# Delta rule in a decoder layer: products of raw keys, key norms applied as row and column factors

## The reference

```python
mixed = silu(causal_conv1d(hidden @ w_qkv, conv_w))
q, k, v = split(mixed)
q, k = l2norm(q), l2norm(k)              # x * rsqrt(sum(x*x) + 1e-6), per token and head
beta, g = sigmoid(b), -exp(A_log) * softplus(a + dt_bias)
for t in range(512):                     # per batch and value head, S is 128 x 128
    S = S * exp(g_t)
    delta = (v_t - k_t @ S) * beta_t
    S = S + outer(k_t, delta)
    o_t = (q_t * 128**-0.5) @ S
core = o * rsqrt(mean(o*o) + 1e-6) * norm_weight * silu(z)
x = x + core @ w_out
```

## Time and profile before

| | |
|---|---|
| median of 3 runs | 3336.58 us (3334.99 to 3337.07) |
| the profiled execution, its own time | 3335.47 us |
| its span in the profile | 3333.6 us |
| instructions | 59535 |
| busy TensorE (PE) | 3238.8 us, 97% of the span |
| busy VectorE (DVE) | 2414.8 us, 72% |
| busy GpSimd (POOL) | 1863.5 us, 56% |
| busy ScalarE (ACT) | 1541.4 us, 46% |
| DMA, mean | 70 GB/s |

### The profile page before, as it was taken

One profiled execution on the slowest core, in us unless ns is written; L12 is line 12 of the kernel. 1 busy time (PEld: TensorE's weight loads), 2 busy tenths in 40 slices (PEclk: granted clock), 3 DMA queues, 4 the chain that ended last, 5 costly groups with the idle time before them and its releaser, 6 DMA issues. The chain is left out here.

```text
span 3333.6 us, 59535 instructions
## 1 busy us (share of the span) xinstructions
PE 3238.8 (97%) x20832; PEld 2152.7 (65%) x20832; DVE 2414.8 (72%) x3622; ACT 1541.4 (46%) x4983; POOL 1863.5 (56%) x1824
## 2 busy tenths in 40 slices
PE   5899999999999999999999999999988999999999
PEld 2577777777777777777777777777764444454444
DVE  6799999999999999999999999999940011034453
ACT  2455556555655555556555655565631000011232
POOL 2677777777777777777777777777740000011132
PEclk8999999999999999999999999999989999999999
DMA  2122322323232323322332233223215222211001
GB/s 101 42 61 77 70 71 58 77 64 71 64 77 64 71 65 71 73 65 61 78 71 69 58 78 67 67 66 77 75 52 211 76 101 101 76 38 64 0 13 38
DMA packets 373958, 231.85 MB, mean 70 GB/s; under 512 B 290304, under 2 KB 323200, under 8 KB 368128
## 3 DMA queue, kind: packets, MB, share of 16 engines
q1 hardware_dynamic: 372368, 220.97, 25.4%
q10 hardware_dynamic: 1296, 7.08, 0.5%
HBM read 156.39 MB, written 71.57 MB: 68 GB/s over the span
## 5 line engine op out<-in xcount | busy, mean ns | idle before, releaser
L722 PE MATMUL acc<-xT,wc 128*128 128x512 f32 x2048 | 935.8, 600 | 2.8 <-PEq L111 2.0
L722 PEld LDWEIGHTS acc<-xT,wc 128*128 128x128 f32 x2048 | 370.2, 191 | 373.2 <-issue 372.5
L1007 DVE SCALAR_TENSOR_TENSOR d_conv<-acc,wc,d_conv 128x511 f32<-128x511 f32 (+2 forms) x768 | 567.0, 738 | 42.7 <-ACT d_conv L1176 33.5
L735 PE MATMUL acc<-wc,xT 128*128 128x256 f32 x2048 | 473.4, 384 | 0.0
L735 PEld LDWEIGHTS acc<-wc,xT 128*128 128x128 f32 x2048 | 379.1, 190 | 46.2
L622 POOL TENSOR_TENSOR d_bf<-d_kks,d_gam 128x512 f32<-128x512 f32 x128 | 160.3, 1273 | 317.9 <-ACT d_kks L1222 317.9
L1530 PE MATMUL acc<-t_area 128*128 128x512 f32 x768 | 332.5, 592 | 1.0 <-ACT t_area L1979 1.0
L1035 DVE STREAM_TRANSPOSE d_em<-d_dm 128x1024 f16<-128x1024 f16 x256 | 314.5, 1229 | 2.2
L2036 POOL TENSOR_SCALAR t_veps<-t_mv 128x1 f32<-128x1 f32 x32 | 9.7, 303 | 546.1 <-DVE t_mv L1775 546.1
L1042 DVE TENSOR_TENSOR d_zm<-d_tz,cons 128x512 f16<-128x512 f32 x384 | 259.1, 675 | 52.7 <-PE d_tz L790 47.7
L1765 DVE TENSOR_TENSOR t_x<-acc,t_x 128x512 f32<-128x512 f32 x16 | 11.1, 692 | 392.4 <-PE acc L1530 392.4
(11 more groups left out here) (227 smaller groups left out, 7084.5 us busy)
## 6 DMA issues: line engine op xcount, KB each, us to landing
d_decay<-decay_rows SPq DMA_DIRECT2D x64, 512.0 KB, 5.2
v_rows<-d_vb SPq DMA_DIRECT2D x256, 128.0 KB, 2.3
d_vn<-v_rows SPq DMA_DIRECT2D x64, 512.0 KB, 3.6
core_rows<-d_ob SPq DMA_DIRECT2D x1024, 32.0 KB, 1.7
t_area<-core_rows SPq DMA_DIRECT2D x30, 1024.0 KB, 4.8
wc<-in_w SPq DMA_DIRECT2D x96, 256.0 KB, 3.3
t_x<-in_x SPq DMA_DIRECT2D x4, 1024.0 KB, 9.6
t_area<-in_wout ACTq DMA_DIRECT2D x2, 2048.0 KB, 13.4
```

The lines of the kernel that those rows point to most:

```text
L722: last = nc.tensor.matmul(bank(TILE[j])[:, :], wtile(j, k), xT[:, k, r % B * S:(r % B + 1) * S], start=k == 0, stop=k == KT - 1)
L735: last = nc.tensor.matmul(bank(f"z{j}")[:, i * GV * P:(i + 1) * GV * P].rearrange("p (h n) -> p h n", h=GV), xT[:, k, r % B * S + (2 * j + ...
L1007: nc.vector.scalar_tensor_tensor(c[:, d:S], bank(TILE[j])[:, 0:S - d], tap(j, KS - 1 - d), c[:, d:S], ALU.mult, ALU.add).then_inc(taps, 1)
```

## The change

It lets the keys be used raw where they stand with channels on partitions, and puts the norms in afterwards:

- silu writes raw keys straight into `kT`, which has four buffers now; `k_turn` reads them there. `normal_k` still makes `khat` (for `grow`). `khat_turn` and `copy_kT` are gone.
- `kk` and `kq` are products of raw keys. Their copies out of PSUM are four of 128 columns, each scaled per row by `rk` (four buffers now), in place of one of 512 columns without a scale.
- B needs the norm of the column's token too. SP stores `rk` to DRAM (`store_row`) and loads it back to all 128 partitions as a row of 512 (`load_row`, 256 KB), and GpSimd multiplies `kks` by it in place (`column_scale`) ahead of `b_full`.
- `read_k` uses raw keys, so GpSimd makes `rt` = -decay times `rk` (`state_scale`, 128 x 8), which `residual` takes as its factor.
- TensorE's order: `kk` of unit n stands where `kq` of unit m stood, and `kq` where `khat_turn` stood. The place of `kk`, between `grow` and `level_d(m, 3)`, is empty. ScalarE's order: `copy_kk` stands where `copy_kq` stood, and `copy_kq` where `copy_kk` stood. The banks follow.

```diff
@@ -320,9 +320,9 @@
         cb, decay, ident = many("conv", 2, [P, S]), many("decay", 2, [P, GV, S]), sb("ident", [P, S])
-        kraw, vraw, vn = sb("kraw", [P, S]), sb("vraw", [P, GV, S]), many("vn", 2, [P, NC, GV * NC, 32])
+        krow, vraw, vn = sb("krow", [P, S]), sb("vraw", [P, GV, S]), many("vn", 2, [P, NC, GV * NC, 32])
         khat = many("khat", 2, [P, S])
-        qT, kT = many("qT", 3, [P, S]), many("kT", 3, [P, S])
+        qT, kT = many("qT", 3, [P, S]), many("kT", 4, [P, S])
         tabm = many("tabm", 4, [P, QN * GV * NC])
...
@@ -429,12 +430,12 @@
 
-        RING_ORDER = ("q", "k", "z1", "v1", "k_turn", "z0", "kq", "v0", "khat_turn", "q_turn", "kk")
-        RING_BANK = {"q": 1, "k": 2, "z1": 0, "v1": 1, "k_turn": 2, "z0": 0, "kq": 2, "v0": 0, "khat_turn": 2, "q_turn": 2, "kk": 1}
+        RING_ORDER = ("q", "k", "z1", "v1", "k_turn", "z0", "kk", "v0", "kq", "q_turn")
+        RING_BANK = {"q": 1, "k": 2, "z1": 0, "v1": 1, "k_turn": 2, "z0": 0, "kq": 1, "v0": 0, "q_turn": 2, "kk": 2}
         RING_FREED = {"k": (taps, "taps", 2), "q": (taps, "taps", 5), "v0": (taps, "taps", 8), "v1": (taps, "taps", 11),
                       "z0": (z_silued, "z_silued", 0), "z1": (z_silued, "z_silued", 1),
-                      "k_turn": (khat_ready, "squares", NC - 1), "khat_turn": (kT_ready, "once", 0), "q_turn": (q_squares, "squares", NC - 1),
-                      "kk": (kk_copied, "once", 0), "kq": (kqs_ready, "once", 0)}
+                      "k_turn": (khat_ready, "squares", NC - 1), "q_turn": (q_squares, "squares", NC - 1),
+                      "kk": (kk_copied, "squares", NC - 1), "kq": (kqs_ready, "squares", NC - 1)}
         CONV_ORDER = ("k", "v1", "v0", "q")
...
@@ -494,8 +495,12 @@
                     next_weights(n, 3)
+                if project:
+                    store_row(n)
                 if invert:
                     store_v(back(n, 1))
+                if project:
+                    load_row(n)
                 if recur:
...
@@ -546,6 +551,15 @@
 
+            def store_row(n):
+                sp.wait_ge(rk_ready, at(n, 2, 2))
+                sp.dma_start(row_dram[n[1] % 2], rk[n[1] % 4][:, :]).then_inc(row_moved, 16)
+
+            def load_row(n):
+                sp.wait_ge(row_moved, at(n, 32, 16))
+                wait(sp, kk_ready, count(n, 1))
+                sp.dma_start(krow[:, :], bc(row_dram[n[1] % 2].rearrange("p c -> (p c)"), P, 0)).then_inc(row_moved, 16)
+
             def store_o(s):
...
@@ -579,7 +593,19 @@
                 wait(pool, khat_ready, at(back(n, 1), NC, NC))
-                nc.gpsimd.tensor_tensor(rk[:, :], rkt[:, :], cons[:, C_POW:C_POW + NC], ALU.pow).then_inc(rk_ready, 1)
+                nc.gpsimd.tensor_tensor(rk[n[1] % 4][:, :], rkt[:, :], cons[:, C_POW:C_POW + NC], ALU.pow).then_inc(rk_ready, 1)
+
+            def state_scale(n):
+                pool.wait_ge(tab_ready, count(n))
+                pool.wait_ge(rk_ready, at(n, 2, 2))
+                nc.gpsimd.tensor_tensor(rt[n[1] % 4][:, :].rearrange("p (h c) -> p h c", h=GV),
+                                        tab(n, Q_NEGDEC).rearrange("p (h c) -> p h c", h=GV), bc(rk[n[1] % 4][:, :], GV),
+                                        ALU.mult).then_inc(rt_ready, 1)
+
+            def column_scale(n):
+                pool.wait_ge(kk_copied, at(n, NC, NC))
+                pool.wait_ge(row_moved, at(n, 32, 32))
+                nc.gpsimd.tensor_tensor(by_chunk(kks), by_chunk(kks), krow[:, :].rearrange("p (i c) -> p c i", c=NC), ALU.mult).then_inc(kk_ready, 1)
 
...
@@ -616,13 +642,13 @@
             def b_full(n, h):
-                pool.wait_ge(kk_copied, count(n))
+                pool.wait_ge(kk_ready, count(n))
                 pool.wait_ge(gams_ready, nth(n, "gams_ready", h))
                 wait(pool, bl_ready, nth(n, "bl_ready", h, 1))
                 nc.gpsimd.tensor_tensor(bf[h][:, :], kks[:, :], gam[h][:, :], ALU.mult).then_inc(bf_ready, 1)
 
             def p_full(m, h):
-                pool.wait_ge(kqs_ready, count(m))
+                pool.wait_ge(kqs_ready, at(m, NC, NC))
                 pool.wait_ge(gamc_ready, nth(m, "gamc_ready", h))
...
@@ -689,12 +715,14 @@
                     k_norm(n)
+                    state_scale(n)
                 if finish:
                     o_norm(f)
                     o_gate(f, 0)
                     o_gate(f, 1)
                 if project:
                     gate_strict(n, 0)
+                    column_scale(n)
                     b_full(n, 0)
...
@@ -750,12 +778,7 @@
                 ring_free(n, "k_turn")
-                turn(bank("k_turn"), kraw, k_turned)
-
-            def khat_turn(n):
-                pe.wait_ge(khat_ready, at(n, NC, NC))
-                ring_free(n, "khat_turn")
-                turn(bank("khat_turn"), khat[n[1] % 2], khat_turned)
+                turn(bank("k_turn"), kT[n[1] % 4], k_turned)
 
...
@@ -763,15 +786,15 @@
             def kk(n):
-                pe.wait_ge(kT_ready, count(n))
+                pe.wait_ge(silued, nth(n, "silued", 0))
                 ring_free(n, "kk")
-                products(bank("kk"), kT[third(n)], kT[third(n)], kk_done)
+                products(bank("kk"), kT[n[1] % 4], kT[n[1] % 4], kk_done)
 
             def kq(m):
-                pe.wait_ge(kT_ready, count(m))
+                pe.wait_ge(silued, nth(m, "silued", 0))
                 pe.wait_ge(silued, nth(m, "silued", 1))
                 ring_free(m, "kq")
-                products(bank("kq"), kT[third(m)], qT[third(m)], kq_done)
+                products(bank("kq"), kT[m[1] % 4], qT[third(m)], kq_done)
 
...
@@ -963,15 +986,16 @@
                     head_start(s, 1)
+                if project:
+                    kk(n)
+                if invert:
+                    level_z(m, 2)
+                if project:
+                    tile(n, 2)
+                if invert:
+                    level_d(m, 2)
                 if invert:
                     kq(m)
-                    level_z(m, 2)
-                if project:
-                    tile(n, 2)
-                if invert:
-                    level_d(m, 2)
-                if project:
-                    khat_turn(n)
                 if recur:
...
@@ -983,8 +1007,6 @@
                     head_start(s, 4)
-                if project:
-                    kk(n)
                 if invert:
...
@@ -1063,7 +1085,8 @@
                 dve.wait_ge(ks_s, at(s, 3, c))
-                nc.vector.scalar_tensor_tensor(by_block(chunk(rr, h)), by_block(chunk(psa, h)), tab(s, Q_NEGDEC, h, c),
+                dve.wait_ge(rt_ready, count(s))
+                nc.vector.scalar_tensor_tensor(by_block(chunk(rr, h)), by_block(chunk(psa, h)), rt[s[1] % 4][:, h * NC + c:h * NC + c + 1],
                                                vn[s[1] % 2][:, :, h * NC + c, :], ALU.mult, ALU.add).then_inc(r_ready, 1)
...
@@ -1178,11 +1201,11 @@
                 if j == 0:
-                    wait(act, k_turned, count(n, 1))
+                    wait(act, ks_s, at(back(n, 4), 3, 3))
                 if j >= 2:
                     wait(act, v_flipped, count(n, 1))
                 v = vraw
-                out = (kraw[:, :], qT[third(n)][:, :], v[:, 0, :], v[:, 1, :])[j]
+                out = (kT[n[1] % 4][:, :], qT[third(n)][:, :], v[:, 0, :], v[:, 1, :])[j]
                 nc.scalar.activation(out, conv_of(TILE[j])[:, :], ACT.Silu).then_inc(silued, 1)
...
@@ -1207,10 +1230,6 @@
 
-            def copy_kT(n):
-                act.wait_ge(khat_turned, count(n))
-                nc.scalar.activation(kT[third(n)][:, :], bank("khat_turn")[:, :], ACT.Copy).then_inc(kT_ready, 1)
-
             def b_high(n, h):
...
@@ -1218,8 +1237,10 @@
                 act.wait_ge(kk_done, count(n))
+                act.wait_ge(rk_ready, at(n, 2, 2))
                 wait(act, bf_ready, at(back(n, 1), GV, GV))
-                nc.scalar.activation(kks[:, :], bank("kk")[:, :], ACT.Copy).then_inc(kk_copied, 1)
+                for c in range(NC):
+                    nc.scalar.activation(chunk(kks, c), chunk(bank("kk"), c), ACT.Copy, scale=rk[n[1] % 4][:, c:c + 1]).then_inc(kk_copied, 1)
 
...
@@ -1232,12 +1253,13 @@
                 for c in range(NC):
-                    nc.scalar.activation(chunk(khat[n[1] % 2], c), chunk(bank("k_turn"), c), ACT.Copy, scale=rk[:, c:c + 1]).then_inc(khat_ready, 1)
+                    nc.scalar.activation(chunk(khat[n[1] % 2], c), chunk(bank("k_turn"), c), ACT.Copy, scale=rk[n[1] % 4][:, c:c + 1]).then_inc(khat_ready, 1)
 
             def copy_kq(m):
                 act.wait_ge(kq_done, count(m))
                 wait(act, p_ready, at(back(m, 1), GV, GV))
-                nc.scalar.activation(kqs[:, :], bank("kq")[:, :], ACT.Copy).then_inc(kqs_ready, 1)
+                for c in range(NC):
+                    nc.scalar.activation(chunk(kqs, c), chunk(bank("kq"), c), ACT.Copy, scale=rk[m[1] % 4][:, c:c + 1]).then_inc(kqs_ready, 1)
 
...
@@ -1318,18 +1340,17 @@
```

(16 more changed lines are left out.)

11 lines of the change are left out of this document (6 added, 5 removed).

## The result

The changed kernel takes 3342.43 us in the median of 19 runs (3340.01 to 3343.75), the kernel before 3334.57 in 19 runs beside them (3330.95 to 3338.97). The ratio is 1.0022, with an interval from 1.0015 to 1.0029: slower, as forecast, by 0.22%, and inside the range. The size is not what was forecast: +7.9 us measured, where the sum had +13.3.

A forecast was written before the change was run, and what follows sets the result against it. TensorE was taken to bound the kernel, with VectorE 2.7 us behind in a slot. 62 slots at +0.19 us (11.8) and the ends (1.5) added 13.3 us to 3335.5; forecast median 3350 us, range 3337 to 3362.

The forecast's parts named there:

- the sum: Total predicted change: 11.8 us for the slots and 1.5 us for the ends, 13.3 us slower.
- the hole: TensorE idle between grow(s, 1) and read_k(s, 2), waiting for VectorE's state: 1.32 us needed, 0.68 filled, 0.64 us every slot.
- rival 2: A wait of about 0.45 us instead of 0.64 cancels the saving: 3338 us, within 0.2%; chance 0.12.
- The order of TensorE's steps: With kk gone from between grow and read_k, 0.68 us of work there can't cover the 1.32 us needed.
- The usual slot: Three of four recurrence slots, 36.81 us before; forecast 0.19 us longer, at 37.0 us.
- 62 slots alike: Every slot from n = 2 to 63 was taken to lengthen by 0.19 us, 11.8 us in all.
- end slots: Slots where a key head ends and weights are replaced, one in four; 37.40 us before, forecast 37.6.
- The ends: Start of the pipeline: in slot 0 TensorE waits for a bank normal_k frees; taken as +1.5 us, bounds 0 to 3.
- The pages: Skill-page claims: weight loads pulled ahead, making read_k 0.43 us; strided reads cost half more, making column_scale 1.9 us.
- The whole 0.47 off: Rival: no wait forms at read_k(s, 2), so 62 x 0.47 = 29 us go, 3308 us; chance 0.14.
- Hole and saving cancel: Rival: slack elsewhere in the slot, as at ScalarE's DMA wait, takes up the shift: 3338 us; chance 0.12.
- The late row: Rival: the norms' row reaches GpSimd late, delaying b_full and TensorE's bank: 3380 to 3610 us; chance 0.05.

The follow-up runs named there:

- `p_full` twice: The changed kernel with GpSimd's p_full(s, 0) computed twice, so that it runs while VectorE starts its first scan; 3346.34 us, ratio 1.0042.
- `kq` late: The changed kernel with kq(m) moved from ahead of solve(s, 1) to behind grow(s, 1); 3316.01 us, ratio 0.995.

## Why the prediction was wrong, and what in it was right

The direction, the range and the hole came out as forecast; the size did not. Of the 13.3 us that the sum had, 7.0 came, and the 3342.4 measured lies nearer to the 3338 of rival 2 than to 3350. The step that failed is the one on the 62 slots, below.

- **The order of TensorE's steps.** Right. That `kk` no longer lies between `grow` and `read_k`, and that 0.68 us can't cover 1.32, is what happened (1.31 measured in two kernels). Filling the hole was free, moving 0.47 us into it brought 0.32 a slot, moving 0.9 brought 0.55, and making the hole in the kernel before cost 0.84.
- **The usual slot.** Forecast +0.19, measured +0.25. The row of `read_k` shows 0.42 us idle where the forecast said about 0.6: the view counts from the end of `level_d(m, 3)`'s row of 0.41 us (1080.80). From start to start the hole is nearly as forecast, 1081.22 less 1080.39 and the 0.23 that `level_d` needs: 0.60, where the forecast had 0.64. What the forecast missed is 0.08 us of `kq`: 0.98 us behind the float16 products of `level_d`, where I had taken `kk`'s 0.90 behind `grow`. That adds 46 x 0.05 to 0.06, 2.5 us, to the sum.
- **62 slots alike.** This step failed. The sum took +0.19 in all 62 slots, so it held that the end slots keep their wait of 0.6 us and become 37.6. They became 37.10 in the mean, 15 x 0.53 = 8 us less than the forecast (37.44 and 0.19). I had seen the wait in the earlier trace rows and put it down to a DMA, as the view names it, without asking what had started the DMA. It was started by VectorE, behind a scan that ran against `p_full`; and that `b_full` starts 3.5 us earlier I had worked out, and called it worth nothing, "since TensorE did not wait for it". For `b_full` that is so. But GpSimd's next operations came earlier too, and the scan found GpSimd idle: 1.21 us where the forecast left it, without naming it, at 2.09. `p_full` twice gave 0.3 us of the wait back, and the scan behind the `convolve` took it away in 12 of 15 end slots of the kernel before. The end slots shown bear out the chain: from `close` to the end of the first scan it is 25.95 us in the kernel before, 25.97 with `p_full` twice and 25.37 with `kq` late, and these slots take 37.37, 37.34 and 36.82. The changed kernel has 25.32; by these rows its chain would need an estimated 36.8, less than the 37.07 that TensorE with its hole takes. With the scan at 2.09 it would have been 26.20 and the end slot an estimated 37.6, so the forecast for them hung on the scan alone.
- **The ends.** Forecast +1.5, measured 1.6 at the start and 0.1 behind, but -0.7 in the last two periods. That the 1.6 agrees says little: in the traces of the seven other kernels made from the changed one the same point lies from 0.4 us earlier to 2.9 later than in the kernel before.
- **The sum.** 11.8 + 1.5 forecast; measured 11.2 - 5.2 - 0.7 + 1.7 = 7.0 on the spans. A further 2.0 us of the forecast's distance is that it counted from a median of 3336.58, where the 19 runs of the comparison gave 3334.57.
- **The pages.** By the weight load that is pulled ahead (the Trainium skill, "TensorE: Matmul & The Clock Gate", section "Step-by-step: what each phase is for") `read_k` was to take 0.43 us. It takes 0.53, with the load starting when the wait ends, although its weights, the keys, were ready: the pull-ahead did not reach past the wait, and the row was right. By the Trainium skill's "GPSIMD Engine Reference", section "7. Performance pitfalls for Q7 kernels", `column_scale` was to take an estimated 1.9 us; it takes 1.53, a fifth more than the 1.27 of `b_full`. The wait for the row is 18.3 us in all, 14.2 of it in the first three slots.
- **The rivals.** The whole 0.47 off: fell, the hole is there; it would have needed 0.9 us behind `grow`, and even with that the slot is 0.29 shorter and not 0.47. Of the missing 0.18, 0.11 lies from `solve` to the tile in the kernel with `kq` late (4.46 us, before 4.35), again in the group behind `level_d`. The other 0.08, a hundredth more than is missing, lies ahead of `solve`, which starts 0.31 us behind `level_d(m, 2)` and not 0.23, at 1063.38, when VectorE's `residual` ends at 1063.33; the transposes had covered that. Hole and saving cancel: the hole was 0.60 and not 0.45, and slack at the DMA's wait did not take up the shift, since the scan, and with it the chain to `attend`, starts 0.26 us later too. The wait went by the shorter scan, and that gave back nearly half of what the usual slots lost. So this rival's number came close by luck. The late row: fell, without the transfers the time is the same. Two figures there are off by their own terms: the 3308 of the first rival is 3309, and the 3610 of the third is 3617 (3350 and 62 x 4.3).

## What to carry to other kernels

When a reordering takes a step away, look at what else it stood in front of: a group between a producer and its reader on the engine that sets the pace may be worth more as cover than its own length, so take the length out at another place, or move something else in. When a wait names a DMA, follow it back to what issued it before calling it fixed. And an engine off the path that gets its work done earlier can still change the time, by what it no longer runs beside.
